# Gated cross-attention with a routed expert layer: another order of heads, turns and last experts, and 192 rows contracted as 128 and 64

## The reference, cut

```python
def _xattn(query, key, value):                  # query (8,112,256); key = value (8,375,192)
    q, k, v = heads(query @ Wq + bq), heads(key @ Wk + bk), heads(value @ Wv + bv)   # 16 heads of 16
    attn = softmax(einsum('bhqd,bhkd->bhqk', q, k) * SCALE)
    return unheads(einsum('bhqk,bhkd->bhqd', attn, v)) @ Wo + bo

def _ffn(x):                                    # 8 experts, 112 places each, first come
    logits = x @ wg
    ...
    return combine(gate, experts(dispatch(x)))  # gate = the top probability

x = x + tanh(g_xattn) * _xattn(layernorm(x), ctx, ctx)
x = x + tanh(g_ffn) * _ffn(layernorm(x))
```

## Time and profile before

| | us |
|---|---|
| device time, median of 3 runs | 185.61 (184.95 to 186.53) |
| the profiled execution | 185.55 |
| its span | 183.8 |
| TensorE busy | 169.8 |
| VectorE busy | 128.7 |
| GpSimd busy | 86.4 |
| ScalarE busy | 80.7 |

### The profile page before, as it was taken

How to read it: one execution, slowest core, us unless ns; L and a number is a source line. 1 busy time by engine, 2 the same in 40 slices (tenths; PEclk the granted TensorE clock), 3 DMA queues, 4 the chain that set the end, 5 groups by cost and what they waited for, 6 DMA issues and landing times.

```text
span 183.8 us, 4666 instructions
## 1 busy us (share of the span) xinstructions
PE 169.8 (92%) x1799; PEld 119.6 (65%) x1799; DVE 128.7 (70%) x325; ACT 80.7 (44%) x174; POOL 86.4 (47%) x112
## 2 busy tenths in 40 slices
PE   7999979997899999999999999799689989999992
PEld 2557446674587768868766886666467876468740
DVE  5878787838278859858875988895876547755642
ACT  2114131377546817645671764356357760013100
POOL 7297948346991198563027007631040057304650
PEclk9999999999999999999999999999999999999998
DMA  5995838687375357616737532886050005387220
GB/s 153 303 259 123 187 86 208 164 197 186 92 167 136 128 129 168 211 52 156 208 100 168 162 115 69 194 255 220 0 154 4 0 23 180 117 239 199 65 61 25
DMA packets 26029, 26.04 MB, mean 142 GB/s; under 512 B 9677, under 2 KB 24409, under 8 KB 26008
## 3 DMA queue, kind: packets, MB, share of 16 engines
q1 hardware_dynamic: 24322, 23.04, 48.0%
q0 software_dynamic: 864, 2.07, 3.7%
q10 hardware_dynamic: 822, 0.64, 1.3%
HBM read 8.89 MB, written 5.06 MB: 76 GB/s over the span
## 4 chain that ended last, share of the span: by engine, by line
PE 65%; DVE 13%; SPq 5%; DMA 5%; issue 4%; ACT 4%; POOL 3%; DVEq 0%; ACTq 0%; POOLq 0%
PE pj L500 9%; PE pv L576 8%; PE sT L561 7%; PE pj L517 6%; PE sc L531 6%; PE sT L832 4%; PE sc L832 3%; PE pj L813 3%; DVE nmax L1097 3%; DMA ctx_sb<-in_ctxT 3%; PE pj L509 3%; PE misc L590 3%; SPq L364 2%; DMA x_sb<-in_x 2%; SPq L358 2%
## 5 line engine op out<-in xcount | busy, mean ns | idle before, releaser
L1097 DVE TENSOR_REDUCE nmax<-sc 112x1 f32<-112x375 f32 x112 | 58.4, 539 | 23.6 <-PE sc L531 19.6
L945 ACT ACTIVATE prob<-sT 128x448 f32<-128x448 f32 (+1 forms) x96 | 50.0, 545 | 38.1 <-PE sT L561 37.5
L561 PE MATMUL sT<-q,k 128*128 128x112 bf16 x384 | 31.7, 213 | 2.6 <-ACT prob L945 2.0
L1412 POOL TENSOR_SCALAR ve<-mv 112x1 f32<-112x1 f32 (+2 forms) x12 | 2.9, 238 | 66.2 <-DVE mv L1167 58.9
L531 PE MATMUL sc<-k,q 126*128 126x375 bf16 x104 | 31.7, 325 | 1.5 <-DVE nmax L1097 1.3
L561 PEld LDWEIGHTS sT<-q,k 128*128 128x128 bf16 x384 | 24.3, 98 | 13.2 <-ACT prob L945 4.8
L500 PE MATMUL pj<-ctx_sb,wk_sb 128*128 128x375 f32 x64 | 23.3, 485 | 0.9 <-DVE rest_q L1085 0.6
L576 PE MATMUL pv<-prob,v_sb 128*32 128x112 f32 (+1 forms) x768 | 21.8, 261 | 0.0
L576 PEld LDWEIGHTS pv<-prob,v_sb 128*32 128x32 f32 (+1 forms) x768 | 18.0, 110 | 3.6 <-issue 2.7
L517 PE MATMUL pj<-wv_sb,ctx_sb 128*128 128x256 f32 (+1 forms) x72 | 18.9, 384 | 0.0
L1428 POOL TENSOR_TENSOR parts_k<-rest_k,parts_k 128x750 bf16<-128x750 f32 x8 | 12.5, 1562 | 7.1 <-ACT parts_k L899 7.1
(11 more groups left out here) (178 smaller groups left out, 276.6 us busy)
## 6 DMA issues: line engine op xcount, KB each, us to landing
k<-parts_k SPq DMA_DIRECT2D x48, 187.5 KB, 3.0
q<-parts_q SPq DMA_DIRECT2D x48, 56.0 KB, 2.5
ctx_sb<-in_ctxT SPq DMA_DIRECT2D x8, 281.2 KB, 4.8
wT_sb<-in_wT SPq DMA_DIRECT2D x8, 256.0 KB, 3.0
slots<-xin SPq DMA_DIRECT2D x1, 1799.0 KB, 8.3
xin<-slots SPq DMA_DIRECT2D x8, 112.9 KB, 2.2
xin<-slots SPq DMA_DIRECT2D x8, 112.0 KB, 2.8
out<-rows SPq DMA_DIRECT2D x1, 672.0 KB, 4.3
```

The source lines that it names most:

```text
L561: mm = pe.matmul(st[n % 2][:, j * NQ:(j + 1) * NQ], k6_flat[:, b % RING, from_key:from_key + CK], q6[:, b % RING, h, :], start=True, stop= ...
L945: nc.scalar.activation(prob[0:rows_here, n, :], st[n % 2][0:rows_here, 0:4 * NQ], ACT.Exp, scale=SCALE).then_inc(s_p, 1)
L1097: nc.vector.tensor_reduce(nmax[:, h:h + 1], scores_bank(b, i)[0:NQ, 0:NK], axis=AX.X, op=ALU.max, negate=True).then_inc(s_max, 1)
```

## The change

- Context and weights of keys and values are laid as 128 rows and 64 rows, and the 64 twice, on rows 0 to 63 and 64 to 127. `project_k(b, 0)` has the two full products of both halves of the heads, `project_k(b, 1)` the two remainders, one on the upper and one on the lower half of the array's rows, into two PSUM banks. `first_keys` does the same. Values of batches 2 to 7: full products for the first two thirds of the keys (place 7), for the last third in two halves of the columns (place 9), then the remainders in two pairs (place 10). Batches 0 and 1 do the remainders one at a time. A load of context grows from 281.2 KB to 375 KB.
- The ones below the context go, and their memsets. The key bias is added where keys are read (two `Identity` copies with a bias, two `scalar_tensor_tensor`, 375 columns each, in place of one of 750). The value bias goes through Wo once, ahead of step 2, and is added to bo there; the adding of bo to x on GpSimd moves from step 1 to step 2.
- Heads 0 to 3 of batch t + 1 are done at places 9 to 11 of step t, so a step begins with head 4. The maxima are split at place 8 and turned at place 9 (before 9 and 11). The late order follows, with the turning of batch 6 ahead of units 4 and 5 of batch 5 and units 6 to 11 in a row. Copying all values waits for all of them.
- Head: keys' weights load ahead of x; both first keys stand ahead of the turning of x; the values of batch 0 stand behind its queries; VectorE prepares the first set of queries ahead of normalising batches 1 and 2; the memsets stand earlier.
- End: the last two experts of the last batch are two calls in two banks, and each is summed when it is there.

```diff
-KC = DC // 2
+FULL, REST = 128, DC - 128
...
-HEADS = ((0, 1), (2, 3), (4, 5), (6, 7), (), (8, 9), (10,), (11, 12), (), (13, 14, 15), (), ())
+HEADS = ((4, 5), (6, 7), (8,), (9,), (), (10, 11), (12,), (13, 14), (15,), (), (), ())
+NEXT_HEADS = (((),) * 9 + ((0,), (1,), (2, 3)), ((),) * 10 + ((0, 1), (2, 3)))
...
-PV_AT, WO_AT, X2T_AT, LOGITS_AT, MAX_AT = (0, 6), 5, 1, 3, (8, 11)
+PV_AT, WO_AT, X2T_AT, LOGITS_AT, MAX_AT = (0, 6), 5, 1, 3, (8, 9)
...
-REST_AT, TURN_AT, SUMS_AT, SCALE_AT, BACK_AT, ADD_AT, STAT_AT, SPLIT_AT = (5, 5), 1, 1, 2, 3, 7, (9, 11), (6, 9)
+REST_AT, TURN_AT, SUMS_AT, SCALE_AT, BACK_AT, ADD_AT, STAT_AT, SPLIT_AT = (5, 5), 1, 1, 2, 3, 7, (9, 11), (6, 8)
...
-    return (REST_HEADS if t == 1 else HEADS)[n]
+    own = (REST_HEADS if t == 1 else HEADS)[n]
+    return [(t, h) for h in own] + [(t + 1, h) for h in at(NEXT_HEADS, t)[n]]
...
+            def halves_of_keys(weights, ctx, m):
+                these = slice(m * REST, (m + 1) * REST)
+                return pe.matmul(pj[:, m, 0:NK], weights[these, 1, m * 128:(m + 1) * 128], ctx[these, 1, :],
+                                 start=False, stop=True, tile_position=(m * REST, 0))
+            def project_k(b, part):
...
+                ctx = ctx_sb[:, b % CRING, :, :]
+                for m in range(2):
+                    if part == 0:
+                        if b == 1:
+                            pe.wait_ge(s_kfe, m + 1)
+                        pe.matmul(pj[:, m, 0:NK], wk_sb[:, 0, m * 128:(m + 1) * 128], ctx[:, 0, :],
+                                  start=True, stop=False)
+                    else:
+                        mm = halves_of_keys(wk_sb, ctx, m)
+                        if b == 1:
...
+            def project_v(b, n):
+                ctx = ctx_sb[:, b % CRING, :, :]
+                last_keys = slice(2 * CK, NK)
+                for a in range(2):
+                    keys = slice(a * CK, (a + 1) * CK)
+                    cols = slice(a * 128, (a + 1) * 128)
+                    these = slice(a * REST, (a + 1) * REST)
+                    if n == 0:
+                        pe.matmul(pj[:, a, 0:D], ctx[:, 0, keys], wv_sb[:, 0, :], start=True, stop=False,
+                                  skip_group_check=True)
+                    elif n == 1:
+                        pe.matmul(pj[0:SIZES[2], a, D:D + 128], ctx[:, 0, last_keys], wv_sb[:, 0, cols],
+                                  start=False, stop=False, skip_group_check=True)
+                if n == 2:
+                    for a in range(2):
+                        cols = slice(a * 128, (a + 1) * 128)
+                        these = slice(a * REST, (a + 1) * REST)
+                        pe.matmul(pj[0:SIZES[2], a, D:D + 128], ctx[these, 1, last_keys],
+                                  wv_sb[these, 1, cols], start=False, stop=True,
+                                  tile_position=(a * REST, 0), skip_group_check=True)
+                    for a in range(2):
+                        keys = slice(a * CK, (a + 1) * CK)
+                        these = slice(a * REST, (a + 1) * REST)
+                        pe.matmul(pj[:, a, 0:D], ctx[these, 1, keys], wv_sb[these, 1, :],
+                                  start=False, stop=True, tile_position=(a * REST, 0),
+                                  skip_group_check=True).then_inc(s_v, 1)
+
+            def value_bias_through_wo():
+                pe.wait_ge(s_bvw, 1)
+                for g in range(2):
+                    mm = pe.matmul(misc[0:NQ, 0:D], onorm[:, g, :], wo_sb[:, g, :],
+                                   start=(g == 0), stop=(g == 1))
+                mm.then_inc(s_bvo, 1)
...
             first_keys(0)
+            first_keys(1)
             pe.wait_ge(s_ident, 1)
             turn_xn(0)
...
-            pe.wait_ge(s_wv, 16)
-            project_v(0, 0)
-            project_v(0, 1)
+            project_k(0, 0)
             first_scores(2)
-            project_k(0, 0)
+            project_k(0, 1)
             first_scores(3)
-            project_k(0, 1)
             project_q(0, 0)
             project_q(0, 1)
+            pe.wait_ge(s_wv, 16)
+            project_v_plainly(0, 0)
+            project_v_plainly(0, 1)
...
+                    pe.wait_ge(s_mrows, 2)
+                    value_bias_through_wo()
...
-            late_scores(6, 0, 1)
+            late_scores(6, 4, 5)
             half_of_probs_v(4, 1)
-            late_scores(6, 2, 3)
+            late_scores(6, 6, 7)
             pe.wait_ge(s_rest, 2 * B)
             pe.wait_ge(s_ve, 2 * LATE)
             project_v(6, 0)
-            late_scores(6, 4, 5)
+            late_scores(6, 8, 9)
             pe.wait_ge(s_mrows, LATE)
             turn_xn2(3)
             late_units(5, 0, 1)
-            late_scores(6, 6, 7)
+            late_scores(6, 10, 11)
             project_v(6, 1)
             logits(3)
-            late_scores(6, 8, 9)
+            late_scores(6, 12, 13)
             through_wo(4)
             late_units(5, 2)
-            late_scores(6, 10, 11)
+            late_scores(6, 14, 15)
             project_v(6, 2)
             late_units(5, 3)
-            late_scores(6, 12, 13)
+            turn_max(6)
             late_units(5, 4, 5)
-            late_scores(6, 14, 15)
+            late_scores(7, 0, 1)
             half_of_probs_v(5, 0)
+            late_scores(7, 2, 3)
             late_units(5, 6, 7)
-            turn_max(6)
-
-            late_scores(7, 0, 1)
-            late_units(5, 8, 9)
-            late_scores(7, 2, 3)
-            late_units(5, 10, 11)
+
+            late_units(5, 8, 9, 10, 11)
             half_of_probs_v(5, 1)
...
+            def last_dense(e):
+                if e == 6:
+                    pe.wait_ge(s_xinTe, E)
+                at = dense_at(1, e)
+                for c in range(2):
+                    pe.matmul(at, x2T[:, LAST, c, :], wT_sb[:, e, c, :], start=(c == 0), stop=False)
+                pe.matmul(at, pick[:, e, :], be_rows[:, :], start=False, stop=True).then_inc(s_dense, 1)
...
+            act.dma_start(wkh_sb, wkh.rearrange("c p n -> p c n")).then_inc(s_wkh, 16)
             act.dma_start(x_sb[:, 0, :], x[0, :, :]).then_inc(s_x, 16)
-            act.dma_start(wkh_sb, wkh.rearrange("c p n -> p c n")).then_inc(s_wkh, 16)
+            act.dma_start(bkc_sb[:, :], bkc).then_inc(s_bkc, 16)
...
-                leave(parts_k[:, b % 2, 0, :, :], k_psum(b), s_hi)
+                for m in range(2):
+                    ins = nc.scalar.activation(parts_k[:, b % 2, 0, m, :], pj[:, m, 0:NK], ACT.Identity,
+                                               bias=bkc_sb[:, m:m + 1])
+                ins.then_inc(s_hi, 1)
...
-                act.wait_ge(s_v, 2 * b + 1)
+                act.wait_ge(s_v, 2 * b + (1 if b < 2 else 2))
...
+            act.wait_ge(s_bkc, 16)
             leave_first_keys(0)
+            leave_first_keys(1)
             leave_xnT(0)
-            leave_first_keys(1)
...
-                nc.vector.tensor_tensor(rest_k[:, :, :], k_psum(b), parts_k[:, b % 2, 0, :, :],
-                                        ALU.subtract).then_inc(s_rest, 1)
+                for m in range(2):
+                    ins = nc.vector.scalar_tensor_tensor(rest_k[:, m, :], pj[:, m, 0:NK], bkc_sb[:, m:m + 1],
+                                                         parts_k[:, b % 2, 0, m, :], ALU.add, ALU.subtract)
+                ins.then_inc(s_rest, 1)
...
-            normalise(1, 1, 3)
             dve.wait_ge(s_qf, 1)
             dve.wait_ge(s_bqc, 16)
-            for n in range(4):
+            first_queries_of(0)
+            normalise(1, 1, 3)
+            for n in range(1, 4):
...
+                        dve.wait_ge(s_bvc, 16)
+                        nc.vector.tensor_copy(onorm[:, :, :], bvc_sb[:, :].unsqueeze(2).to_broadcast([128, 2, NQ]))\
+                            .then_inc(s_bvw, 1)
+                    if t == 2 and n == 0:
                         dve.wait_ge(s_tanh, 1)
                         dve.wait_ge(s_bo, 16)
+                        dve.wait_ge(s_bvo, 1)
+                        link(nc.vector.tensor_tensor(bo_sb[:, :], misc[0:NQ, 0:D], bo_sb[:, :], ALU.add))
...
-            late_max(6, 4, 5, 6, 7, 8, 9, 10)
+            late_max(6, 8, 9, 10, 11, 12, 13)
             add_x(4)
-            late_max(6, 11)
+            late_max(6, 14)
             sums_2(4)
-            late_max(6, 12)
+            late_max(6, 15)
             variance_2(4)
-            late_max(6, 13, 14, 15)
             split_max(6)
+            leave_max_rows(6)
             late_max(7, 0)
...
+                if t == 2:
                     pool.wait_ge(s_xn, 3)
                     pool.wait_ge(s_tbo, 1)
-                if t < LAST:
+                    add_output_bias(0)
+                if 2 <= t < LAST:
...
-        "ctxT": np.asarray(ctx_768).transpose(2, 0, 1).reshape(2, KC, B, NK),
+        "ctxT": rest_twice(np.asarray(ctx_768).transpose(2, 0, 1)),
```

(12 more changed lines are left out.)

136 lines of the change are left out of this document (68 added, 68 removed).

## The result

The changed kernel takes 196.13 us (median of 4 runs, 195.09 to 197.27) against 185.56 for the kernel before (4 runs): a ratio of 1.057, interval 1.049 to 1.065. Forecast were 188.1 and at most 190.3.

A forecast was written before the change was run, and what follows sets the result against it. TensorE bounds the full steps and a chain of waits the late step; head +0.2, step 1 +0.2, bias +0.9, steps 2 to 4 +1.2, step 5 -0.2, late +0.8, end -0.55 make +2.55: 188.1 us, range 182.0 to 190.3.

The forecast's parts named there:

- Head: Kernel start: queries up to 1.7 earlier, chain behind them 1.7 longer; taken as +0.2, bounds -1.8 and +1.2.
- Keys in halves: Key projection: four full passes and a pair of 0.98 replace eight passes, gaining 0.29 us a batch.
- rival C: Key pairs: switches cost nothing, a pair takes 0.63 instead of 0.98; 185.7 us, chance 0.10 within noise and 0.02 faster.
- Rival E: Halves don't run side by side: keys and values each 0.65 a batch more, some +7; 195 us, chance 0.02.
- B: Rival: head and late step gain (-1.8, -1.9), steps don't; 183.4 us, chance 0.07.
- Values in halves: Value projection, batches 2 to 7: TensorE passes fall from 2.6 to 2.29, gaining 0.3 us a batch.
- Heads and turns: End of a step: TensorE idles 0.5 before turning maxima and 0.44 before score 3; full step 16.04, +0.4.
- Rival A: Full steps: VectorE's reductions come in time, TensorE stays full; 182.4 us, chance 0.22 faster and 0.02 within noise.
- F: Rival, full steps: VectorE already sets the step, which keeps 15.64 whatever TensorE saves; 186.5 us, chance 0.04.
- D: Rival, context loads: the larger context lands late, +0.6 in three steps; 189.9 us, chance 0.05.
- Biases: Value bias through Wo: 0.9 on the path at step 2's front; key bias, some 0.15 on ScalarE and VectorE, hidden.
- Late: Late step: VectorE holds batch 6's turning 1.0, then units run at ScalarE's pace; +0.8, bounds -1.9 and +1.5.

The follow-up runs named there:

- the last kernel: Kernel with head, steps and late step ordered as before, keys in pairs, but values contracted in two passes of 128 rows again: ratio 0.989 to the kernel before.
- table early: Changed kernel with one small activation ahead of the first key copies, so ScalarE loads its table before the keys are ready: 192.65 us.
- head as before: Changed kernel with the head's order undone on all engines; halves, biases, steps and end as changed: 191.25 us.
- turn later: Kernel with the head as before, with the maxima turned two places later, after the last unit of the step: 189.18 us.
- tanh times bias: Changed kernel with tanh times bias as a product of two tensors in place of a tensor and a scalar: 196.49 us.
- filler: Changed kernel with eight products of unused results in TensorE's idle time before the first queries, table load left late: 193.90 us.
- bias in the tail: Kernel with the head as before, tanh times bias as two-tensor product, value bias product moved into step 1's tail: 190.43 us.

## Why the prediction was wrong, step by step

**The step that failed is "Head".** The prediction's own sign of being wrong came: the first step starts over 1 us later. It said that the head goes "in pace with the score groups", bounds -1.8 and +1.2, and took +0.2. Measured from first keys to the first turned maxima: 24.85 against 19.53, +5.3. In place of VectorE's reductions, the chain ahead of them decided:
- first queries +2.3: 1.35 by the table load (5.06 to 3.71 without), the rest by x being turned behind both parts of the keys and copied behind two key copies (undone only together, with fills and normalisation). I had listed these copies as standing ahead of x, and not followed who waits for x. The load was in no row that I quoted: in the trace of before it runs beneath other work, and the change adds a wait ahead of it, with two things queued behind. The Trainium skill, ScalarE: Activation LUTs, section What ACT_TABLE_LOAD costs, gives 1283 ns for the load; the rows show 1.28.
- the lower clock, +1.5 to the first scores, and in this execution 1.6 more in the second slow stretch, between the turned maxima and keys 4. I never asked what the clock does when TensorE idles, since it was 1.00 throughout before.
- +1.5 to the turned maxima: 1.0 by the values behind the queries, which my bound of +1.2 held, and about 0.6 by values in passes of 128 and 64 rows in turn: 8 passes start within 2.47 (27.69 to 30.16, rows above), where eight of 128 took 1.73 before:

```profile
32.21 1.89 PE L517 MATMUL pv<-wv_sb,ctx_sb 128*128 128x256 f32 x8
33.94 0.48 PE L531 MATMUL sc<-k,q 126*128 126x375 bf16 x2
```

I had the price of a change of form, 0.10 from the earlier trace rows, and charged it to the pairs alone; batches 0 and 1 change at every second pass, four times in these eight, for 0.74, or 0.19 a change. How much of that is the change and how much a weight load that is no longer covered was not separated. The Trainium skill, TensorEngine Tiling (Array Packing), section Key Properties, says that switching the tiling mode drains TensorE: the rows agree that a change costs time.

**Keys in halves: right.** Forecast were 0.98 for a pair and 0.29 a batch. The pair's four passes take 0.83 (93.31 to 94.14), and going over to them 0.10 more; with the values whole a step is 0.34 under the 15.63 of before. The 0.63 that the prediction worked out by the Trainium skill, TensorE: Matmul & The Clock Gate, section Part 3: Packing small matmuls, didn't come: rival C is out. Rival E too, by the kernel with remainders one at a time; and B, as head and late step lost.

**Values in halves: the gain is there, its price was missed.** TensorE's passes fell from 2.65 to 2.20 (2.30 with going over to them; forecast 2.29), but not the time: the copy that waits for all of them holds the next keys. I had seen that wait for batch 7 only, at 0.3 against 0.3; the last batch lost 0.6, and with the values whole again it is back at the 25.3 of before.

**Heads and turns: right.** Forecast idle 0.5 at the turning and 0.44 at the third score; measured from start to start 0.43 and 0.45 in step 4, with the releasers named (rows at 102.97 and 105.21). In step 3 the turning waited 0.94, as VectorE's cast ahead of it took 0.68, to the end of GpSimd's adding of bo, and not the 0.17 of step 4:

```profile
86.14 0.72 POOL L1503 TENSOR_TENSOR x_sb<-x_sb,tbo 112x256 f32<-112x256 f32 x1
...
86.22 0.68 DVE L1179 CAST mparts<-nmax 112x16 bf16<-112x16 f32 x1
...
87.16 0.22 PE L600 MATMUL misc<-ident_b,mparts 112*32 112x112 bf16 x1 [0.77 <-DVE mparts L1181]
...
102.53 0.17 DVE L1179 CAST mparts<-nmax 112x16 bf16<-112x16 f32 x1
```

Steps 3 and 4: 16.32 and 15.80 against the forecast 16.04. Rival A, no waits, is out; so is F, as the last kernel's 15.3 with VectorE at 12.2 shows.

**Loads: right.** No key product waited for context; D is out. Steps 4 and 5 together became 0.1 longer, forecast +0.2.

**Step 1:** of the 3.0 between turned maxima and keys 4, 1.6 are the lower clock and 0.9 the product of the value bias; 0.4 is left, with batch 1's values in it, for the +0.2 forecast.

**Biases: the product right, its neighbour not.** 0.9 forecast, 0.83 to 0.91 measured. Behind it I expected nothing, "up to 1 if the reductions run late": it was 0.7, not by reductions but since VectorE's next operation ended only with a GpSimd fill (a memset). The two extra copies and subtractions for the key bias were not tried alone; what they cost in the head stays open.

**Late: right in its size**, +0.74 for +0.8; of the 1.0 by which VectorE was to hold the turning of batch 6, TensorE's row at 132.38 shows 0.56 of idle time. **End:** the last sum alone at the end as forecast (from the start of the last experts 4.91, before 5.51),

```profile
192.01 0.48 DVE L1452 SCALAR_TENSOR_TENSOR tbo<-sc,mix,tbo 112x256 f32<-112x256 f32 x1
192.78 0.48 DVE L1452 SCALAR_TENSOR_TENSOR tbo<-sc,mix,tbo 112x256 f32<-112x256 f32 x1 [0.29 <-PE sc L904]
```

but the first expert to the end became only 0.16 shorter, as the last experts began 0.44 later in it; the cause of that wasn't tried.

## What to carry to other kernels

Before an instruction is moved ahead at the start of a kernel, follow the first chain to its end with everything that stands on it, also what the old trace shows as hidden: here the table load stood ahead of one wait before the first activation (at 3.39) and behind two (at 8.36). Where TensorE will stand idle after the move, price the clock as well: here 1.35 us more ahead of the first queries brought 1.5 at the lower clock right behind. A smaller product pays by its passes less the changes of form around it and whatever its later end holds; count all three.

## What the hardware showed that I had not expected

- The granted clock of the changed kernel was 1.00 up to 12 us and 0.50 from 13 to 15, after TensorE had idled for 2.32 us; with products of no use in that time it stayed at 1.00. An idle time of 1.51 or 1.52 us in the changed late step left it alone in four profiles (the changed kernel, table early, head as before, turn later), and in three it fell 1 to 2 us later (tanh times bias, filler, bias in the tail). At 33 it fell in one profile behind idle times of 0.47 and 0.32 us and stayed at 1.00 behind the same in another (the rows beside "the table load alone"); with remainders one at a time it fell behind 0.55 and 0.79, where 0.49 and 0.61 did nothing before. What decides is open.
- VectorE's tensor by scalar (f32, 112 x 256) took 2.15 us, to the end of a GpSimd fill, and 0.42 as a product of two tensors beside the same fill. The Trainium skill, SBUF — State Buffer, section Who interferes with whom, says that tensor_scalar can enter a two-port mode, which contends with GpSimd, and that an operation with two SBUF inputs contends only with one that reads SBUF; a fill doesn't read. The rows agree.
